# A decoder layer on one core: score products on 128 rows, probabilities as fp16 subnormals, and the tile loop written out

## The chip, the core and the metric

One core of a Trainium2 chip runs the whole kernel as one launch. Its engines work side by side and meet at semaphores: TensorE (PE, with PEld for its weight loads), VectorE (DVE), ScalarE (ACT), GpSimd (POOL), and SyncE (SP), which here only issues transfers. The metric is the device time of one execution in microseconds, lower being better.

## The reference, cut to what matters

2048 tokens of width 256 go through three sublayers, each behind a layernorm and added to its input: a self-attention across the 16 heads of one token (so its "scores" are 16 x 16 per token), a cross attention of 2048 queries on 2048 context tokens, and a mixture of 8 experts with 2 chosen. The change lies in the cross attention:

```python
q = _fq_sym(q * scale, axis=-1)          # each query's 16 numbers rounded to 127 steps
k = _fq_sym(k, axis=-1)
v = _fq_sym(v, axis=2)
attn = softmax(einsum('bhqd,bhkd->bhqk', q, k))
attn = _fq_unsigned(attn, axis=-1)       # each row rounded to 0..255, the largest is 255
out = einsum('bhqk,bhkd->bhqd', attn, v)
out = out @ Wp + bp
```

## The kernel before, in words

The tokens are cut into 16 tiles of 128. Keys and values of the context are computed, quantised and kept in SBUF once, in the first 119 us. Then every engine runs its own `body(t)` for t = 0 to 17: tile t is in cross attention, while the same body prepares tiles a = t + 2 and n = t + 1 (layernorm, self-attention, queries) and finishes m = t - 1 and o = t - 2 (output projection, experts). A body has 16 steps h, one for each head; which piece of the other tiles goes into which step is written by hand, and every engine takes its pieces strictly in that order.

One head h of tile t passes four engines. PE multiplies the queries with the keys in two halves of 1024 keys (`scores(h, i, t)`, two matmuls of 512 columns each). The operand `queries` holds two heads on top of each other; a head takes 48 rows from row 0 or from row 64 (a number of 16 is split in three bfloat16 parts, so 3 x 16 rows). DVE turns each half into scaled scores with their minimum (`keep_scores`) and makes the exponent's offset (`bias`). ACT takes the exponential (`exp_head`) and writes 0 to 255. SP issues the transposing transfer of that head from `prob` to `prob_t`. After a lag of 5 steps, PE multiplies the turned probabilities of two heads at a time with the values (`times_values`, in the odd steps between the two halves of the scores). `ps_score` has two halves, so PE may start half i of a head when DVE has read the same half of the head before. `score`, `prob` and `prob_t` are rings of 4 heads.

The 8-bit probability is written as the low byte of a 16-bit float whose high byte is that of 1024, so the number read is 1024 + p. The surplus is taken out on PE: `values4` holds sums over four blocks of values, and `neg1024` is a matrix of -1024. For every four blocks there is one matmul with these two beside the four with the probabilities.

POOL has the self-attention of tile a. In body t it works, in this order: `value_products` 2 and 3 of tile n (step 0, 1), `norm_ho` (step 2, waits for `reduce_values` 3, which DVE has in step 3), `rope` (3), `ln_scale(2, m)` (4, waits for DVE's step 6), `score_products` 0 and 1, `ln_scale(1, n)`, `score_products` 2, `choose(m)` (the experts of m, line 516 is its end), `score_products` 3, `shift_scores`, `value_products` 0 and 1. ACT's `route` waits for the end of `choose`. In step 13 it stands behind `keep_queries(n)` and `keep_routed` with `head_exp(a)`, for which POOL's `value_products` wait. DVE's `reduce_scores` 3 of tile a stands in step 13 as well.

The bodies of t = 3 to 12 are a loop with two bodies in it, run five times; those of 0 to 2 and 13 to 17 are written out. In the loop the values that a wait compares with are worked out in registers.

Of the kernel before, what the change touches and what calls it, by code (L numbers as in the profile page):

```python
# [36 lines left out]
F32 = mybir.dt.float32  # L37
BF16 = mybir.dt.bfloat16
F16 = mybir.dt.float16
U8 = mybir.dt.uint8  # L40
# [5 lines left out]
P = 128  # L46
D = 256
# [19 lines left out]
TWO_1024 = float(np.array([1024.0, 1024.0], np.float16).view(np.float32)[0])  # L67


class Tile:  # L70


    def __init__(self, idx, least, par):
        self.idx, self.least, self.par = idx, least, par

    def __add__(self, n):
        return Tile(self.idx + n, self.least + n, (self.par + n) % 2)

    def starts(self):
        return isinstance(self.idx, int) and self.idx == 0  # L80

    def exists(self):
        return not isinstance(self.idx, int) or 0 <= self.idx < T

    def starts(self):
        return isinstance(self.idx, int) and self.idx == 0

    def exists(self):
        return not isinstance(self.idx, int) or 0 <= self.idx < T

    def count(self, n, extra=0):

        return self.idx * n + extra

    def due(self, n, extra=0):

        if isinstance(self.idx, int):
            return self.idx * n + extra if self.idx * n + extra > 0 else None
        assert self.least * n + extra > 0
        return self.idx * n + extra  # L100

    def pairs(self, n, extra=0):

        return (self.idx - self.par) * (n // 2) + extra
# [12 lines left out]


def layer_kernel(nc, a):
    with ExitStack() as ctx:  # L120
# [15 lines left out]
        neg1024 = sb("neg1024", [P, P], F16)  # L136
# [29 lines left out]
        values4 = sb("values4", [P, T // 4, H // 2, 3, HD], F16)  # L166
# [19 lines left out]

        values2 = score[:, 3, 0:NTOK // 2].bitcast(F16).rearrange("p (a g j d) -> p a g j d", g=H // 2, j=2, d=HD)
# [6 lines left out]
        queries = sb("queries", [P, 2, H // 2, P], BF16)  # L194
        k_int = queries[:].rearrange("p r a q -> p (r a q)").bitcast(F32)[:, 0:2 * D].rearrange("p (h d) -> p h d", d=HD)
# [68 lines left out]
        prob_set = sem("prob_set")  # L264
# [16 lines left out]
        values_added = sem("values_added")  # L281
# [32 lines left out]
        q_kept = sem("q_kept")  # L314
        sum_inverted = sem("sum_inverted")
# [36 lines left out]
        def _(sp):  # L352
# [8 lines left out]
            load_x(Tile(0, 0, 0))  # L361
# [12 lines left out]
            load_x(Tile(1, 1, 1))  # L374
# [30 lines left out]
            load_x(Tile(2, 2, 0))  # L405

            sp.wait_ge(v_turned, T // 4)
            over_tiles(sp, body)
# [4 lines left out]
        def _(pool):  # L413
            pool.memset(ones_row[:], 1.0).then_inc(const_made, 1)
            pool.memset(minus_half[:], -0.5).then_inc(const_made, 1)
            pool.memset(neg1024[:], -1024.0).then_inc(const_made, 1)
            pool.memset(values[:, :, :, 1, :].rearrange("p a g d -> p (a g) d"), 0.0).then_inc(zeros_set, 1)
            pool.memset(values4[:, :, :, 1, :].rearrange("p a g d -> p (a g) d"), 0.0).then_inc(zeros_set, 1)
            pool.wait_ge(const_made, 3)
# [191 lines left out]
            first, second = Tile(0, 0, 0), Tile(1, 1, 1)  # L611
# [12 lines left out]
            pool.wait_ge(k_split, T // 2)  # L624
            pool.memset(prob[:, 2:4].bitcast(F32), TWO_1024).then_inc(prob_set, 1)
# [7 lines left out]
            ln_scale(0, Tile(2, 2, 0))  # L633
# [3 lines left out]
            over_tiles(pool, body)  # L637
# [3 lines left out]
        def _(act):  # L641
# [9 lines left out]
            def high_part_of_keys(u):  # L651
# [5 lines left out]
                if u == 0:  # L657
                    act.wait_ge(rows_set, 3)
# [77 lines left out]
            def keep_queries(t):  # L736
# [4 lines left out]
                act.copy(queries[:, t.par].rearrange("p a q -> p (a q)"), bank_bf[5]).then_inc(q_kept, 1)  # L741

            def exp_head(h, t):
# [5 lines left out]
                if h == 2 and t.starts():  # L749
                    act.wait_ge(prob_set, 1)  # L750
# [4 lines left out]
                act.activation(prob[:, s, :].bitcast(U8)[:, 0::2], score[:, s, :], ACT.Exp,  # L755
# [97 lines left out]
            first, second = Tile(0, 0, 0), Tile(1, 1, 1)  # L853
# [25 lines left out]
            over_tiles(act, body)  # L879
# [3 lines left out]
        def _(dve):  # L883
            def quantise_keys(u):
# [3 lines left out]
                step = Tile(u, u, 0)  # L888
# [62 lines left out]
            def round_values():  # L951
# [13 lines left out]

            def add_values():

                dve.wait_ge(values_ready, T // 4)
                dve.wait_ge(k_product, T // 2)
                dve.wait_ge(vt_product, T // 2)  # L970
                v = values[:].rearrange("p (a b) g j d -> p a b g j d", b=2)
                for j in range(0, 3, 2):
                    dve.tensor_tensor(values2[:, :, :, j // 2, :].rearrange("p a g d -> p a g d"), v[:, :, 0, :, j, :],
                                      v[:, :, 1, :, j, :], ALU.add).then_inc(values_added, 1)
                dve.wait_ge(values_added, 2)
                v = values2.rearrange("p (a b) g j d -> p a b g j d", b=2)
                for j in range(2):
                    dve.tensor_tensor(values4[:, :, :, 2 * j, :], v[:, :, 0, :, j, :], v[:, :, 1, :, j, :], ALU.add
                                      ).then_inc(values_added, 1)
# [696 lines left out]
```

## Time and profile before

| | |
|---|---|
| median of 3 runs | 1199.38 us (1195.58 to 1200.67) |
| the profiled execution, its own time | 1197.12 us |
| its span, first to last instruction | 1195.3 us |
| PE matmul busy | 945.0 us (79%) |
| DVE busy | 977.3 us (82%) |
| ACT busy | 743.7 us (62%) |
| POOL busy | 754.0 us (63%) |
| mean granted TensorE clock | 0.774 of 2.4 GHz |

A busy share is an average over the whole span. No engine is at 100%, so the waits have to be read: which engine waited for which, and where in a tile. The granted clock of a stretch is 1.00 at 2.4 GHz and 0.50 at 1.2 GHz.

### The profile page before, as it was taken

To read this page: it belongs to the slowest core of one execution; us is meant where nothing else is said; L and a number is where in the kernel's file an instruction comes from. 1 tells how busy PE (TensorE), PEld (TensorE's weight loads), DVE (VectorE), ACT (ScalarE), POOL (GpSimd) and SP (SyncE) were. 2 spreads that over 40 slices of the span, in tenths; PEclk is the share of its full clock that TensorE was granted. 3 is DMA by queue.
4 is the path that set the end of the run, shared out by engine and by line. 5 is a ranking of instruction groups with operands and counts; after the bars stand their busy time and mean duration, and the time that the engine had idled before them with its cause. 6 is when DMAs were issued, how large, how long until landed. Compare 5 with 4: busy or idle time off the path is not lost. (4 is left out here: it accounts for less than half of the span.)

```text
span 1195.3 us, 25897 instructions
## 1 busy us (share of the span) xinstructions
PE 945.0 (79%) x8256; PEld 516.1 (43%) x8256; DVE 977.3 (82%) x1944; ACT 743.7 (62%) x971; POOL 754.0 (63%) x794
## 2 busy tenths in 40 slices
PE   6765678989896868888797978787787869788874
PEld 3434233544453434444444444444444434444443
DVE  5986979888897969888798879798797979788762
ACT  2443546666777665676667766666557677668562
POOL 6537787767767675777677667767677777711011
PEclk9876667768688877787786868887687979677687
DMA  6001577769787867697896977687687968679780
GB/s 206 1 36 40 99 135 132 127 118 168 125 151 116 147 117 123 127 132 136 126 168 116 152 115 140 117 146 127 114 147 124 168 121 152 121 136 144 132 146 10
DMA packets 541061, 148.24 MB, mean 124 GB/s; under 512 B 534130, under 2 KB 538868, under 8 KB 540532
## 3 DMA queue, kind: packets, MB, share of 16 engines
q1 hardware_dynamic: 540916, 146.44, 69.8%
q8 instruction: 74, 1.21, 0.4%
q14 instruction: 71, 0.58, 0.1%
HBM read 10.09 MB, written 2.10 MB: 10 GB/s over the span
## 5 line engine op out<-in xcount | busy, mean ns | idle before, releaser
L1071 DVE TENSOR_SCALAR_CACHE_REDUCE score<-ps_score,q_neg 128x1024 f32<-128x1024 f32 x512 | 640.8, 1279 | 110.1 <-PE ps_score L1423 95.2
L755 ACT ACTIVATE prob<-score,exp_bias 128x2048 uint8<-128x2048 f32 x256 | 512.4, 2002 | 148.9 <-DVE exp_bias L1081 148.5
L1423 PE MATMUL ps_score<-keys,queries 48*128 48x512 bf16 x1024 | 369.4, 457 | 105.6 <-DVE score L1071 93.2
L1445 PE MATMUL ps_pv<-prob_t,values 128*32 128x128 f16 x4096 | 213.8, 260 | 0.0
L547 POOL TENSOR_TENSOR product<-hs_exp,v_tok 128x1024 f32<-128x1024 f32 x64 | 183.0, 2860 | 36.8 <-ACT hs_exp L728 36.7
L553 POOL TENSOR_TENSOR folded<-product 128x512 f32<-128x512 f32 x128 | 163.2, 1275 | 43.6 <-POOL product L547 33.8
L1445 PEld LDWEIGHTS ps_pv<-prob_t,values 128*32 128x32 f16 x4096 | 182.8, 119 | 0.0
L1423 PEld LDWEIGHTS ps_score<-keys,queries 48*128 48x128 bf16 x1024 | 61.8, 99 | 256.2 <-DVE score L1071 186.7
L547 POOL TENSOR_TENSOR product<-qk_rot 128x1024 f32<-128x1024 f32 x64 | 150.7, 2355 | 2.6 <-issue 1.4
L1441 PE MATMUL ps_pv<-neg,values 128*32 128x128 f16 x1024 | 136.1, 259 | 11.5 <-DMA prob_t<-prob 11.3
L784 ACT ACTIVATE routed_both<-normed,routed_gate 128x256 bf16<-128x256 f32 x124 | 52.6, 496 | 89.6 <-POOL routed_gate L516 89.6
L1441 PEld LDWEIGHTS ps_pv<-neg,values 128*32 128x32 f16 x1024 | 62.6, 115 | 89.6 <-issue 89.6
L429 POOL TENSOR_SCALAR var_eps<-mean_var 128x1 f32<-128x1 f32 x48 | 12.1, 252 | 106.8 <-DVE mean_var L990 83.5
L1490 PE MATMUL ps<-ident_bf,routed_both 128*128 128x128 bf16 x256 | 27.3, 271 | 46.8 <-ACT routed_both L784 27.5
L1296 PEld LDWEIGHTS ps<-routed_both,w 128*128 128x128 bf16 x512 | 40.4, 122 | 40.6 <-issue 34.3
L1081 DVE TENSOR_SCALAR exp_bias<-low 128x1 f32<-128x1 f32 x256 | 52.9, 206 | 4.0
L998 DVE TENSOR_REDUCE hs<-folded 128x64 f32<-128x256 f32 x64 | 26.4, 414 | 34.8 <-POOL folded L558 34.8
L558 POOL TENSOR_TENSOR folded<-folded 128x256 f32<-128x256 f32 x64 | 47.5, 743 | 11.4 <-POOL folded L553 11.4
L1296 PE MATMUL ps<-routed_both,w 128*128 128x128 bf16 x512 | 53.1, 269 | 1.9 <-DVE early L1134 1.8
L755 ACT ACTIVATION_READ_ACCUMULATOR prob<-score,exp_bias 128x1 f32 x256 | 48.5, 189 | 0.0
L460 POOL TENSOR_TENSOR ho_n<-ho,hs_inv 128x256 f32<-128x256 f32 x16 | 10.0, 622 | 60.7 <-DVE ho L1020 60.7
L707 ACT COPY normed_t<-ps 128x256 f32<-128x256 f32 x48 | 17.6, 367 | 46.5 <-PE ps L1301 46.5
(136 smaller groups left out, 1276.8 us busy)
## 6 DMA issues: line engine op xcount, KB each, us to landing
prob_t<-prob SPq DMA_TRANSPOSE x256, 4.5
prob_t<-in_w SPq DMA_DIRECT2D x3, 1024.0 KB, 4.8
x_in<-in_x SPq DMA_DIRECT2D x16, 128.0 KB, 2.7
score<-in_cond_t SPq DMA_DIRECT2D x4, 512.0 KB, 7.1
out<-x_out SPq DMA_DIRECT2D x16, 128.0 KB, 2.4
w_qkv<-in_w_qkv SPq DMA_DIRECT2D x1, 768.0 KB, 4.1
early<-in_w_kv SPq DMA_DIRECT2D x1, 512.0 KB
w_s<-in_w_s SPq DMA_DIRECT2D x3, 128.0 KB
```

Source lines behind the costliest of these rows:

```text
L547: pool.tensor_tensor(product[:, r], a_, b_, ALU.mult).then_inc(multiplied, 1)
L553: pool.tensor_tensor(folded[:, r], product[:, r, :, :, 0:HD // 2], product[:, r, :, :, HD // 2:HD], ALU.add).then_inc(fold_done, 1)
L558: pool.tensor_tensor(folded[:, r, :, :, 0:HD // 4], folded[:, r, :, :, 0:HD // 4], folded[:, r, :, :, HD // 4:HD // 2], ALU.add).then_inc( ...
L755: act.activation(prob[:, s, :].bitcast(U8)[:, 0::2], score[:, s, :], ACT.Exp, bias=exp_bias[:, s:s + 1], scale=-1.0, accum_out=prob_sum[:, ...
L784: act.activation(routed[:, e, :], normed[:, 2, :], ACT.Copy, scale=routed_gate[:, e:e + 1]).then_inc(routed_done[i], 1)
L1071: dve.tensor_scalar(score[:, s, HALF * i:HALF * i + HALF], ps_score[:, i].rearrange("p b k -> p (b k)"), q_neg[:, t.par, h:h + 1], None, A ...
L1081: dve.tensor_scalar(exp_bias[:, s:s + 1], low[:, s, 0:1], low[:, s, 1:2], LN255, ALU.min, ALU.add).then_inc(bias_ready, 1)
L1296: mm = pe.matmul(out, lhs[c], rhs[c], start=start and c == 0, stop=stop and c == C - 1)
L1423: mm = pe.matmul(ps_score[:, i, b, :], queries[lo:lo + 3 * HD, t.par, h // 2, :], keys[lo:lo + 3 * HD, h // 2, k0:k0 + KEYS], start=True, ...
L1441: pe.matmul(out[j], beside_zeros(values4, i, h + j), neg1024[:], start=(i == 0 and first), stop=False)
L1445: mm = pe.matmul(out[j], beside_zeros(values, 4 * i + b, h + j), prob_t[:, (h + j) % RING, 4 * i + b, :], start=False, stop=(i == T // 4 - ...
L1490: mm = pe.transpose(bank_bf[6 + i][:, P * j:P * j + P], routed[:, EG * i + e, P * c:P * c + P], ident_bf[:])
```

## The change

Three things are changed, all in how the cross attention is carried out; the layer's result is the same function.

1. `queries` gets a further dimension j: block j holds the queries of head 2a + j in its own 64 rows, and zeros in the other 64 rows, set once. A score product takes all 128 rows of `queries` and of `keys`. `keep_queries` is two copies of 64 rows in place of one of 128.
2. The exponential writes a 16-bit integer 0 to 255, which read as a 16-bit float is the subnormal p x 2^-24; `w_p` is multiplied by 2^24 once. `neg1024`, `values4`, `add_values` and their 1024 matmuls go.
3. `over_tiles` is a Python loop over all 18 bodies, so no engine branches back and every wait compares with a constant.

```diff
@@ over_tiles
-def over_tiles(eng, body):
-    for t in range(3):
-        body(Tile(t, t, t % 2))
-    with eng.Fori(3, T - 4, 2) as t:
-        body(Tile(t, 3, 1))
-        body(Tile(t + 1, 4, 0))
-    for t in range(T - 3, T + 2):
-        body(Tile(t, t, t % 2))
+def over_tiles(body):
+    for t in range(T + 2):
+        body(Tile(t))
@@ buffers
-        queries = sb("queries", [P, 2, H // 2, P], BF16)
+        queries = sb("queries", [P, 2, H // 2, 2, P], BF16)
@@ gpsimd
-            pool.wait_ge(k_split, T // 2)
-            pool.memset(prob[:, 2:4].bitcast(F32), TWO_1024).then_inc(prob_set, 1)
+            pool.wait_ge(k_chain, 6 * (T // 2))
+            pool.memset(queries[:].rearrange("p r a j q -> p (r a j q)").bitcast(F32), 0.0).then_inc(rows_cleared, 1)
@@ keep_queries
-                act.copy(queries[:, t.par].rearrange("p a q -> p (a q)"), bank_bf[5]).then_inc(q_kept, 1)
+                if t.starts():
+                    act.wait_ge(rows_cleared, 1)
+                for j in range(2):
+                    rows = slice(P // 2 * j, P // 2 * j + P // 2)
+                    act.copy(queries[rows, t.par, :, j, :], bank_bf[5][rows, :].rearrange("p (a q) -> p a q", q=P)
+                             ).then_inc(q_kept, 1)
@@ exp_head
-                act.activation(prob[:, s, :].bitcast(U8)[:, 0::2], score[:, s, :], ACT.Exp,
+                act.activation(prob[:, s, :].bitcast(U16), score[:, s, :], ACT.Exp,
@@ round_values
-                    dve.tensor_scalar(w_p[:, c, :], w_p[:, c, :], v_scale[:, c:c + 1], None, ALU.mult
+                    dve.tensor_scalar(w_p[:, c, :], w_p[:, c, :], v_scale[:, c:c + 1], 1.0 / UNIT, ALU.mult, ALU.mult
@@ vector, tile 0, step 0
-                            add_values()
@@ scores
-                    mm = pe.matmul(ps_score[:, i, b, :], queries[lo:lo + 3 * HD, t.par, h // 2, :],
-                                   keys[lo:lo + 3 * HD, h // 2, k0:k0 + KEYS], start=True, stop=True)
+                    mm = pe.matmul(ps_score[:, i, b, :], queries[:, t.par, h // 2, h % 2, :],
+                                   keys[:, h // 2, k0:k0 + KEYS], start=True, stop=True)
@@ times_values
-                for i in range(T // 4):
-                    for j in range(2):
-                        pe.matmul(out[j], beside_zeros(values4, i, h + j), neg1024[:],
-                                  start=(i == 0 and first), stop=False)
-                    for b in range(4):
-                        for j in range(2):
-                            mm = pe.matmul(out[j], beside_zeros(values, 4 * i + b, h + j),
-                                           prob_t[:, (h + j) % RING, 4 * i + b, :], start=False,
-                                           stop=(i == T // 4 - 1 and b == 3 and last))
+                for i in range(T):
+                    for j in range(2):
+                        mm = pe.matmul(out[j], beside_zeros(values, i, h + j), prob_t[:, (h + j) % RING, i, :],
+                                       start=(i == 0 and first), stop=(i == T - 1 and last))
```

The changes of place can be seen in the order of instructions. On PE, step 5 of tile 0, from the first half of that step's scores (the last two of the four products in the first row are of step 4) to the second half's. Before:

```order
L1296 MATMUL ps<-w_qkv,normed_t 128x256 x2
L1423 MATMUL ps_score<-keys,queries 128x512 x2
L1441 MATMUL ps_pv<-neg,values 32x128 x2
L1445 MATMUL ps_pv<-prob_t,values 32x128 x8
L1441 MATMUL ps_pv<-neg,values 32x128 x2
L1445 MATMUL ps_pv<-prob_t,values 32x128 x8
L1441 MATMUL ps_pv<-neg,values 32x128 x2
L1445 MATMUL ps_pv<-prob_t,values 32x128 x8
L1441 MATMUL ps_pv<-neg,values 32x128 x2
L1445 MATMUL ps_pv<-prob_t,values 32x128 x8
L1423 MATMUL ps_score<-keys,queries 128x512 x2
```

And with the change, at the same place:

```order
L1256 MATMUL ps<-w_qkv,normed_t 128x256 x2
L1382 MATMUL ps_score<-keys,queries 128x512 x2
L1400 MATMUL ps_pv<-prob_t,values 32x128 x32
L1382 MATMUL ps_score<-keys,queries 128x512 x2
L1256 MATMUL ps<-w_qkv,normed_t 128x256 x2
```

The block of products between the two halves goes from 40 matmuls to 32, and nothing else changes its place. On DVE, step 0 of tile 0, from its scores to the scores of step 1. Before:

```order
L1071 TENSOR_SCALAR score,low<-ps_score,q_neg 128x1024 x2
L985 BN_STATS stats<-x_in 128x6
L1081 TENSOR_SCALAR exp_bias<-low 128x1
L973 TENSOR_TENSOR score<-values 128x64x16 x2
L978 TENSOR_TENSOR values<-score 128x32x16 x2
L998 TENSOR_REDUCE hs<-folded 128x64
L963 CAST w<-prob_t 128x2048
```

And with the change:

```order
L1033 TENSOR_SCALAR score,low<-ps_score,q_neg 128x1024 x2
L949 BN_STATS stats<-x_in 128x6
L1043 TENSOR_SCALAR exp_bias<-low 128x1
L962 TENSOR_REDUCE hs<-folded 128x64
L942 CAST w<-prob_t 128x2048
```

The four additions ahead of `reduce_scores` (the first `hs`) are gone.

## Rows read from the trace of the kernel before

**Rows 1.** The page's span, and its granted clock in 40 slices of the span, in tenths.

```profile
span 1195.3 us, 25897 instructions
...
PEclk9876667768688877787786868887687979677687
```

**Rows 2.** Waits of DVE: total us, times, longest; whole span.

```profile
DVE score L1071 <- PE ps_score L1423: 95.2, 88, 5.2
DVE hs L998 <- POOL folded L558: 34.8, 11, 4.4
DVE score L1071 <- issue: 12.9, 8, 5.3
```

**Rows 3.** Timeline at the start of tile 5: start, duration, engine; [idle before].

```profile
448.11 1.28 DVE L1071 TENSOR_SCALAR_CACHE_REDUCE score<-ps_score,q_neg 128x1024 f32<-128x1024 f32 x1 [5.34 <-issue]
...
453.41 0.22 POOL L429 TENSOR_SCALAR var_eps<-mean_var 128x1 f32<-128x1 f32 x1 [5.36 <-issue]
```

**Rows 4.** POOL's timeline: the end of `choose` in bodies 1, 4, 5, 6, 13.

```profile
232.88 0.21 POOL L516 TENSOR_TENSOR routed_gate<-gate 128x8 f32<-128x8 f32 x1 [0.18 <-POOL gate L513]
...
429.11 0.21 POOL L516 TENSOR_TENSOR routed_gate<-gate 128x8 f32<-128x8 f32 x1 [0.18 <-POOL gate L513]
...
497.98 0.21 POOL L516 TENSOR_TENSOR routed_gate<-gate 128x8 f32<-128x8 f32 x1 [0.18 <-POOL gate L513]
...
562.34 0.21 POOL L516 TENSOR_TENSOR routed_gate<-gate 128x8 f32<-128x8 f32 x1 [0.18 <-POOL gate L513]
...
1021.01 0.21 POOL L516 TENSOR_TENSOR routed_gate<-gate 128x8 f32<-128x8 f32 x1 [0.18 <-POOL gate L513]
```

**Rows 5.** ACT's timeline in body 5, from that end of `choose`.

```profile
498.22 1.71 ACT L784 ACTIVATE routed_both<-normed,routed_gate 128x256 bf16<-128x256 f32 x4 [6.13 <-POOL routed_gate L516]
...
505.55 0.99 ACT L741 COPY queries<-ps 128x1024 bf16<-128x1024 bf16 x1
...
507.35 0.42 ACT L728 ACTIVATE hs_exp<-hs 128x256 f32<-128x256 f32 x1
```

**Rows 6.** DVE and POOL, from step 13 of body 5 to step 3 of body 6.

```profile
503.28 0.42 DVE L998 TENSOR_REDUCE hs<-folded 128x64 f32<-128x256 f32 x1 [3.57 <-POOL folded L558]
...
525.88 1.26 POOL L553 TENSOR_TENSOR folded<-product 128x512 f32<-128x512 f32 x1 [0.27 <-POOL product L547]
...
530.22 0.68 DVE L1020 TENSOR_REDUCE ho<-folded 128x64 f32<-128x512 f32 x1
```

**Rows 7.** DVE and PE around step 15 of body 5 and steps 1 and 3 of body 6.

```profile
506.88 0.29 PE L1441 MATMUL ps_pv<-neg,values 128*32 128x128 f16 x2
...
509.13 1.03 PE L1423 MATMUL ps_score<-keys,queries 48*128 48x512 bf16 x2
...
510.20 1.28 DVE L1071 TENSOR_SCALAR_CACHE_REDUCE score<-ps_score,q_neg 128x1024 f32<-128x1024 f32 x1 [1.60 <-PE ps_score L1423]
...
515.08 0.23 PE L1441 MATMUL ps_pv<-neg,values 128*32 128x128 f16 x2 [0.83 <-DMA prob_t<-prob]
...
516.31 0.60 PE L1423 MATMUL ps_score<-keys,queries 48*128 48x512 bf16 x2
...
526.51 1.28 DVE L1071 TENSOR_SCALAR_CACHE_REDUCE score<-ps_score,q_neg 128x1024 f32<-128x1024 f32 x1 [0.96 <-PE ps_score L1423]
...
528.76 1.28 DVE L1071 TENSOR_SCALAR_CACHE_REDUCE score<-ps_score,q_neg 128x1024 f32<-128x1024 f32 x1 [0.96 <-PE ps_score L1423]
```

**Rows 8.** PE in three stretches of bodies 5 and 6: length, busy, granted clock, DMA.

```profile
500.00:510.40 10.40, 8.18 (x68) 0.51 0.67 94
541.10:547.90 6.80, 5.39 (x58) 1.00 1.17 190
551.30:565.00 13.70, 13.51 (x103) 0.50 0.57 115
```

**Rows 9.** DVE's timeline, `add_values` in step 0 of tile 0.

```profile
121.65 2.55 DVE L973 TENSOR_TENSOR score<-values 128x1024 f16<-128x1024 f16 x2
124.23 0.76 DVE L978 TENSOR_TENSOR values<-score 128x512 f16<-128x512 f16 x2
```

**Rows 10.** Waits of DVE from 1026 to 1160 us, the last tiles.

```profile
DVE score L1071 <- PE ps_score L1423: 19.6, 18, 2.7
```

More of the change, by code:

```diff
@@ L65, with __init__ @@
 FLOOR = 1e-8
-TWO_1024 = float(np.array([1024.0, 1024.0], np.float16).view(np.float32)[0])
+UNIT = 2.0 ** -24
 class Tile:
-    def __init__(self, idx, least, par):
-        self.idx, self.least, self.par = idx, least, par
+    def __init__(self, idx):
+        self.idx, self.par = idx, idx % 2
     def __add__(self, n):
-        return Tile(self.idx + n, self.least + n, (self.par + n) % 2)
+        return Tile(self.idx + n)
     def starts(self):
-        return isinstance(self.idx, int) and self.idx == 0
+        return self.idx == 0
     def exists(self):
[L83 to L89, printed above, removed]
+        return 0 <= self.idx < T
     def count(self, n, extra=0):
@@ L609, in body @@
                         value_products(h - 14, a)
-            first, second = Tile(0, 0, 0), Tile(1, 1, 1)
+            first, second = Tile(0), Tile(1)
             ln_scale(0, first)
@@ L850, in body @@
                         exp_head(h, t)
-            first, second = Tile(0, 0, 0), Tile(1, 1, 1)
+            first, second = Tile(0), Tile(1)
             ln_apply(0, x_in[:, 0, :], first)
@@ L877, in _ @@
             keep_values(3)
-            over_tiles(act, body)
+            over_tiles(body)
         @block.vector
@@ L1064, in keep_scores @@
                             dve.wait_ge(k_product, T // 2)
-                        if t.starts() and h == 3:
-                            dve.wait_ge(values_added, 4)
                         if (due := t.due(H, h - RING + 1)) is not None:
@@ L1243, in body @@
                             largest_score(a)
-            first, second = Tile(0, 0, 0), Tile(1, 1, 1)
+            first, second = Tile(0), Tile(1)
             loaded(first)
@@ L1251, in _ @@
             dve.memset(q_parts[:], 0.0).then_inc(rows_set, 1)
-            dve.memset(prob[:, 0:2].bitcast(F32), TWO_1024).then_inc(rows_set, 1)
-            dve.wait_ge(rows_set, 3)
+            dve.wait_ge(rows_set, 2)
             for u in range(T // 2 + 2):
@@ L1287, in _ @@
             reduce_scores(0, second)
-            over_tiles(dve, body)
+            over_tiles(body)
         @block.tensor
@@ L1501, in experts @@
                     if (t + 2).exists():
[L1503 removed]
+                        pe.wait_ge(q_kept, (t + 2).count(2, 2))
                 if i == 1 and j == 1:
@@ L1582, in body @@
                             experts(0, 0, m)
-            first, second = Tile(0, 0, 0), Tile(1, 1, 1)
+            first, second = Tile(0), Tile(1)
             ln_turn(0, first)
@@ L1614, in _ @@
             q_turn(first)
-            over_tiles(pe, body)
+            over_tiles(body)
 def kernel(x, ctx_2048, L0_attn_Wq, L0_attn_Wk, L0_attn_Wv, L0_attn_Wo, L0_xattn_Wq, L0_xattn_bq,
```

63 lines of the change are left out of this document (19 added, 44 removed).

## The prediction

> **What bounds the kernel now.** I read the page first. It has a span of 1195.3 us, and a granted clock that never stays at full or at half for long [rows 1]. DVE is busiest, so I asked next what DVE waits for: 95.2 us for score products of PE in 88 waits, 34.8 us for POOL's folded products in 11 waits, and 12.9 us for "issue", that is for nothing the profile shows, in 8 waits [rows 2]. These three belong to three different limits.
>
> The "issue" waits lie where a loop goes round. At the start of tile 5, DVE stands for 5.34 us, and POOL stands for 5.36 us a little later [rows 3]. The loop runs five times, so there are four such places, at tiles 5, 7, 9 and 11.
>
> For the rest I needed the length of a tile and a marker that is not blurred. I took the end of `choose` on POOL [rows 4]. From body 4 to 5 it is 68.87 us, with a loop-back in it, and from 5 to 6 it is 64.36 us, without one. From body 1 to body 13 it is 788.1 us, 12 tiles. Twelve times 64.4 is 772.8, and the four with a loop-back hold the other 15.3 us; so a loop-back costs 3.8 us net, not 5.3, because other waits of the tile shrink meanwhile.
>
> Then I followed one tile without a loop-back, 64.4 us, from `choose` to `choose` [rows 5, 6]:
> - `choose` ends at 498.2; ACT, which had waited 6.13 us for it, works without a gap to `head_exp` at 507.35: 9.2 us.
> - POOL's last value product is folded at 527.1: 19.8 us.
> - DVE takes it up at 530.2 (`reduce_values` 3, step 3): 3.1 us later. This is the only slack in the ring.
> - From there to the next end of `choose`, 562.5: 32.3 us. In it DVE works for steps 3 to 6 and then POOL without any wait to the end of `choose`.
>
> The reader is to see that POOL and ACT, with 63% and 62% busy, close the ring in all but 3.1 us. DVE confirms it: in step 13 it waits 3.57 us for POOL [rows 6]. The waits of DVE for PE count only as far as they lie between step 13 and step 3: 1.60 us in step 15, and 0.96 and 0.96 in step 3, together 3.5 us [rows 7]. Those in steps 9 and 11 are given back at step 13.
>
> **The loop written out.** Four loop-backs at 3.8 us net: 15 us gained. The bodies that are straight code already (0 to 2, 13 to 17) show no wait for "issue" that matters, so I charge nothing for fetching straight code. Register arithmetic is off: below 0.5 us a tile, taken as nothing.
>
> **Fewer value products.** At the low clock the 40 products between the two halves of a head's scores take 2.25 us (506.88 to 509.13), and at the high clock 1.23 us (515.08 to 516.31) [rows 7]. 32 in place of 40 take off a fifth: 0.45 or 0.25 us. Two such blocks lie on DVE's way between steps 13 and 3 (steps 15 and 3), so 0.9 us a tile at the low clock. Whether a product with subnormal numbers takes longer no row shows. Its bounds are nothing, and a large loss, if it were handled as slowly as fp32, which I price below. I take nothing, since the array gets operands of the same type and shape.
>
> **All 128 rows.** The number of matmuls and their columns stay. So any effect must come by the clock. What do the rows say of it? From 551.3 to 565.0, PE was busy 13.51 of 13.70 us, and had 1.2 GHz; from 541.1 to 547.9 it was busy 5.39 of 6.80 us and had 2.4 GHz [rows 8]. So an engine busy all the time is not enough. The first stretch has mostly score products on 48 rows and value products 32 wide; the second has fp32 products on 128 rows between them. I read this as a grant that depends on how much of the array is in use, so scores on 128 rows should lift it. The pair of score products takes 1.03 us at the low clock and 0.60 at the high one [rows 7].
>
> The Trainium skill says otherwise: by "TensorE: Matmul & The Clock Gate", Part 1, the gate is set by how busy the engine has been. By that rule rows of zeros would lift nothing, and 1024 fewer matmuls would make low stretches more frequent, a result of its own, which is the second of the rivals below.
>
> Where does the lift reach? The two places that count are the worst for it. Between 500.0 and 510.4 PE itself waited (busy 8.18 of 10.40 at 0.51) [rows 8], as it stands behind `choose`, ACT's `route` and DVE's step 13. I expect the clock to come back earlier than now in some tiles and not in others. With the high clock throughout, the 3.5 us go altogether; with none, only 0.9.
>
> **The second copy.** `keep_queries` is one copy of 0.99 us, with `head_exp` behind it [rows 5]. A copy's time goes by the elements of a row, which stay 1024, so the second adds some 1.0 us, and in the ring that is fully on the path: 9.2 becomes 10.2. It is bounded by half a copy if rows count (0) and by 1.0. I take 1.0.
>
> **What stands at the end of it.** The ring is now 10.2 + 19.8 + 32.3 = 62.3 us without any slack: a tile can't be shorter. On DVE's side it is 64.4 less what is recovered of the 3.5: 63.5 with the shorter blocks alone. I take 62.9, midway, since the clock rises in part. For 12 tiles that is 754.8 in place of 788.1 us: 33.3 us gained, the loop-backs included.
>
> **Start and end.** `add_values` takes 3.3 us of DVE ahead of work that POOL waits for [rows 9]; with 0.9 us for the second copy ahead of the first scores, 2.5 us are gained. Behind body 13 POOL has little left, so DVE's waits for PE are on the path: 19.6 us in 18 waits [rows 10]. Of these I take 8: 0.45 for most blocks, and the clock for the rest. The memset that clears `queries` is as large as the one of `prob` that it replaces, and it starts earlier.
>
> **Sum:** 33.3 + 2.5 + 8 = 43.8 us. The profiled execution has 1197.1 us, so 1153.3; it lies 2.3 us under the median of the runs, so I forecast 1155 us.
>
> **The rivals.**
> - *All waits for PE vanish* (the clock is high nearly everywhere). For it: a stretch fully busy was at the low clock, so there is much to win. Against it: PE waits itself in steps 13 to 15. POOL and ACT are then the ring: 12 x 62.3 = 747.6, 40.5 gained, 14 at the end, 2.5 at the start: 1142 us. Chance 0.18.
> - *The grant follows busy time alone.* Then the clock sinks a little as matmuls go, and what the shorter blocks save, low stretches take back: 12 tiles of 64.4 = 772.8, 15.3 gained, 2.5 at the start, 2 at the end: 1179 us. It is spoken against by the busy stretch at half clock [rows 8]. Chance 0.14.
> - *Nothing but the loop is gained, and the copies eat it*: 15 gained, 16 x 1.0 lost: 1200 us beside the median, the change doing nothing for the time. It would need DVE to be late at step 3 for another reason. Chance 0.03.
> - *Slower: straight code stalls at every tile.* If engines that no longer repeat code had to wait for it once in each tile as they now do at a loop-back, 16 times 3.8 us come on top of the forecast: 1216 us. It decides from 2.8 us a tile on (43.8 by 16). Against it: the straight bodies now have no such wait. With it I count products slowed by subnormals: at four times their time a block would grow by 3 us or more, and the time by hundreds. Chance for both 0.05.
>
> The forecast itself has 0.60, with a range of its own from 1146 to 1168.
>
> **How the numbers follow.** A change of up to 0.5% (6 us) can't be told from none here. Faster by more: the first three cases, 0.92. Within it: 0.03. Slower: 0.05. The range leaves out the last two cases and the part of the second that is faster still, so it runs from 1138 (all waits gone and a cheap second copy) to 1180.
>
> **What would show it.** No wait for "issue" of over 1 us on DVE behind the first body. A granted clock between 0.82 and 0.90 over the span; under 0.78 the clock follows busy time alone. DVE's waits for score products at 40 to 60 us. The marker `choose` at steps of 62.3 to 63.5 us; if it is 62.3 in each, POOL and ACT are the bound, and DVE waits for POOL at `ho` in step 3 too. `queries` with 32 copies of about 1 us. DVE's wait for POOL at `hs` stays at 3 to 4 us a tile. I am wrong if tiles come under 62 us, since then the ring has a link that I took as rigid and that isn't, most likely the 32.3 us; or if the value products get longer.

## The result, and the profile after

The changed kernel takes 1142.8 us (median of 4 runs, 1141.5 to 1144.0), the kernel before on the same chip 1198.6 us (4 runs, 1195.6 to 1200.7). The ratio is 0.9536, with a 95% interval from 0.9512 to 0.956: faster by 56 us. The forecast was 1155 us with a range from 1138 to 1180. So the range holds the time; but the forecast's own narrower range (1146 to 1168) doesn't, and the number of the first rival, 1142 us, is the one that was met.

The page of the changed kernel: span, busy time of each engine, and the granted clock in 40 slices.

```profile
span 1140.6 us, 21740 instructions
...
PE 772.9 (68%) x7110; PEld 460.5 (40%) x7232; DVE 947.2 (83%) x1939; ACT 758.7 (67%) x987; POOL 752.4 (66%) x792
...
PEclk9877778979798979879798988898888989898986
```

Against [rows 1], sixes have become eights and nines: the mean granted clock goes from 0.774 to 0.862. DVE, the busiest engine, is busy 30 us less. TensorE's busy time is understated here, since the trace lacks 122 of its 7232 matmuls; exp_first below, with the same matmuls and all of them on record, has 789.1 us, some 156 us less than before.

The waits of DVE: total, times, longest.

```profile
DVE hs L962 <- POOL folded L532: 69.7, 24, 5.1
DVE score L1033 <- PE ps_score L1382: 37.3, 41, 3.2
...
DVE ho L984 <- POOL folded L527: 10.1, 16, 1.0
```

Against [rows 2], the wait for score products falls from 95.2 us to 37.3, and the waits for "issue" of over 1 us are gone. The wait for POOL at `hs` has doubled, from 34.8 to 69.7 us: DVE now arrives in step 13 early in every tile, and what it arrives early for is POOL's chain.

POOL's timeline, the end of `choose` in bodies 1, 4, 5, 6 and 13, as in [rows 4].

```profile
229.25 0.21 POOL L490 TENSOR_TENSOR routed_gate<-gate 128x8 f32<-128x8 f32 x1 [0.18 <-POOL gate L487]
...
416.83 0.20 POOL L490 TENSOR_TENSOR routed_gate<-gate 128x8 f32<-128x8 f32 x1 [0.18 <-POOL gate L487]
...
479.37 0.20 POOL L490 TENSOR_TENSOR routed_gate<-gate 128x8 f32<-128x8 f32 x1 [0.18 <-POOL gate L487]
...
541.90 0.20 POOL L490 TENSOR_TENSOR routed_gate<-gate 128x8 f32<-128x8 f32 x1 [0.18 <-POOL gate L487]
...
979.09 0.21 POOL L490 TENSOR_TENSOR routed_gate<-gate 128x8 f32<-128x8 f32 x1 [0.18 <-POOL gate L487]
```

These rows split the gain. Up to body 1 it is 3.6 us (232.9 to 229.25), over the 12 tiles 38.3 us (788.1 to 749.8), and behind them 12.8 us (174.3 to 161.5 up to the end of the span). All 12 tiles lie between 62.2 and 62.7 us; no tile is longer for a loop-back.

The ring of body 5, first on ACT, then on POOL, then on DVE, as in [rows 5, 6].

```profile
479.61 1.71 ACT L763 ACTIVATE routed_both<-normed,routed_gate 128x256 bf16<-128x256 f32 x4 [6.62 <-POOL routed_gate L490]
...
486.94 2.02 ACT L719 COPY queries<-ps 64x1024 bf16<-64x1024 bf16 x2
488.99 1.01 ACT L770 COPY routed_both<-ps 128x1024 bf16<-128x1024 bf16 x1
489.89 0.42 ACT L702 ACTIVATE hs_exp<-hs 128x256 f32<-128x256 f32 x1
```

```profile
508.38 1.27 POOL L527 TENSOR_TENSOR folded<-product 128x512 f32<-128x512 f32 x1 [0.27 <-POOL product L521]
```

```profile
484.34 0.42 DVE L962 TENSOR_REDUCE hs<-folded 128x64 f32<-128x256 f32 x1 [4.57 <-POOL folded L532]
...
510.05 0.68 DVE L984 TENSOR_REDUCE ho<-folded 128x64 f32<-128x512 f32 x1
```

From the end of `choose` (479.6) to `head_exp` (489.9) it is 10.3 us, to the last folded product (509.65) 19.8, to DVE's `ho` 0.4, and to the next end of `choose` (542.1) 32.1. The sum is 62.5. The slack of 3.1 us has shrunk to 0.4, which is what closes the ring. Body 5 still has some slack; in most of the 12 tiles there is none, and DVE waits 0.4 to 0.6 us for POOL at that `ho`. (In the kernel before, the slack in the 12 tiles ran from nothing, behind one loop-back, to 4.4 us; the 3.1 us are one tile's.)

### The profile page after: what moved, and what is told of

Same layout as the page of the kernel before. It is cut to its first block and busy times, and to the rows that moved or that the text cites. A ratio compares the mean times of both kernels' runs of the same rounds, so it can differ in the third digit from the quotient of the medians.

```text
span 1140.6 us, 21740 instructions
## 1 busy us (share of the span) xinstructions
PE 772.9 (68%) x7110; PEld 460.5 (40%) x7232; DVE 947.2 (83%) x1939; ACT 758.7 (67%) x987; POOL 752.4 (66%) x792
## 5 line engine op out<-in xcount | busy, mean ns | idle before, releaser
L1033 DVE TENSOR_SCALAR_CACHE_REDUCE score<-ps_score,q_neg 128x1024 f32<-128x1024 f32 x512 | 638.0, 1278 | 38.2 <-PE ps_score L1382 37.3
L734 ACT ACTIVATE prob<-score,exp_bias 128x2048 uint16<-128x2048 f32 x256 | 511.4, 1999 | 96.1 <-DVE exp_bias L1043 95.7
L1382 PE MATMUL ps_score<-keys,queries 128*128 128x512 bf16 x902 | 311.8, 424 | 150.2 <-DVE score L1033 127.2
L527 POOL TENSOR_TENSOR folded<-product 128x512 f32<-128x512 f32 x128 | 163.3, 1275 | 40.8 <-POOL product L521 30.5
L1400 PE MATMUL ps_pv<-prob_t,values 128*32 128x128 f16 x4096 | 158.8, 239 | 45.1 <-DMA prob_t<-prob 45.0
L1400 PEld LDWEIGHTS ps_pv<-prob_t,values 128*32 128x32 f16 x4096 | 135.0, 106 | 109.8 <-issue 109.8
L1382 PEld LDWEIGHTS ps_score<-keys,queries 128*128 128x128 bf16 x1024 | 71.4, 104 | 256.9 <-DVE score L1033 221.8
L962 DVE TENSOR_REDUCE hs<-folded 128x64 f32<-128x256 f32 x64 | 26.5, 416 | 69.8 <-POOL folded L532 69.7
L1444 PEld LDWEIGHTS ps<-ident_bf,routed_both 128*128 128x128 bf16 x256 | 21.2, 124 | 86.6 <-ACT routed_both L763 85.3
L1256 PE MATMUL ps<-routed_both,w 128*128 128x128 bf16 x512 | 46.6, 246 | 7.0 <-ACT routed_both L770 5.7
L984 DVE TENSOR_REDUCE ho<-folded 128x64 f32<-128x512 f32 x64 | 42.8, 669 | 10.1 <-POOL folded L527 10.1
L1033 DVE DVE_READ_ACCUMULATOR score<-ps_score,q_neg 128x1 f32 x512 | 42.1, 82 | 0.0
L501 POOL TENSOR_TENSOR qk_sin<-qk,rope_sin 128x256 f32<-128x256 f32 x32 | 27.1, 868 | 17.5 <-ACT qk L689 16.6
## 6 DMA issues: line engine op xcount, KB each, us to landing
w_qkv<-in_w_qkv SPq DMA_DIRECT2D x1, 768.0 KB, 4.3
```

Of the source, the lines that this page charges most:

```text
L527: pool.tensor_tensor(folded[:, r], product[:, r, :, :, 0:HD // 2], product[:, r, :, :, HD // 2:HD], ALU.add).then_inc(fold_done, 1)
L734: act.activation(prob[:, s, :].bitcast(U16), score[:, s, :], ACT.Exp, bias=exp_bias[:, s:s + 1], scale=-1.0, accum_out=prob_sum[:, t.par, ...
L984: dve.tensor_reduce(ho[:, G * j:G * j + G, :], folded[:, j % 2], AX.X, ALU.add).then_inc(reduced, 1)
L1033: dve.tensor_scalar(score[:, s, HALF * i:HALF * i + HALF], ps_score[:, i].rearrange("p b k -> p (b k)"), q_neg[:, t.par, h:h + 1], None, A ...
L1256: mm = pe.matmul(out, lhs[c], rhs[c], start=start and c == 0, stop=stop and c == C - 1)
L1382: mm = pe.matmul(ps_score[:, i, b, :], queries[:, t.par, h // 2, h % 2, :], keys[:, h // 2, k0:k0 + KEYS], start=True, stop=True)
```

## The experiments

Each edit is against the changed kernel unless it says otherwise. Each kernel was timed beside the kernel before on its chip, whose medians were 1200.2 us (first four experiments), 1200.3 (next three) and 1204.9 (last three), so between groups the ratios are to be compared. "12 tiles" is again the time from `choose` of body 1 to that of body 13.

| kernel | median, us | ratio to before, 95% | clock | start, 12 tiles, end, us |
|---|---|---|---|---|
| rows48 | 1178.8 | 0.9825 (0.9774 to 0.9877) | 0.700 | 236.3, 768.0, 174.1 |
| rows64 | 1165.8 | 0.9726 (0.968 to 0.9772) | 0.758 | 234.5, 760.2, 165.2 |
| third_copy | 1159.6 | 0.9665 (0.9617 to 0.9712) | 0.858 | 231.6, 761.1, 166.0 |
| exp_first | 1134.1 | 0.9454 (0.9407 to 0.9501) | 0.872 | 229.7, 740.5, 163.0 |
| straight_only | 1181.5 | 0.9864 (0.9783 to 0.9946) | 0.778 | 232.1, 769.1, 174.3 |
| all_but_rows | 1172.6 | 0.9805 (0.9733 to 0.9878) | 0.706 | 234.1, 762.0, 174.8 |
| change_in_loop | 1180.0 | 0.9838 (0.9771 to 0.9905) | 0.857 | 229.8, 786.7, 163.3 |
| only_tensor_loops | 1174.4 | 0.9757 (0.9713 to 0.9801) | 0.855 | 229.0, 782.5, 161.6 |
| only_tensor_straight | 1167.9 | 0.9714 (0.9672 to 0.9756) | 0.862 | 229.1, 773.6, 161.4 |
| exp_first_in_before | 1198.5 | 0.9966 (0.9937 to 0.9996) | 0.771 | 233.2, 791.4, 170.2 |

**How many rows a score product uses.** The buffer with its zeros and both copies stay; only the slice that the product reads changes, to the 48 rows that hold a head's numbers or to its 64.

```diff
-                    mm = pe.matmul(ps_score[:, i, b, :], queries[:, t.par, h // 2, h % 2, :],
-                                   keys[:, h // 2, k0:k0 + KEYS], start=True, stop=True)
+                    lo = 64 * (h % 2)
+                    mm = pe.matmul(ps_score[:, i, b, :], queries[lo:lo + 48, t.par, h // 2, h % 2, :],
+                                   keys[lo:lo + 48, h // 2, k0:k0 + KEYS], start=True, stop=True)
```

> The changed kernel, but each score product takes only the 48 rows of its own head (queries and keys sliced again), with the new layout, both copies and everything else kept. If the grant of the clock depends on how much of the array is in use: mean granted clock back to 0.76 to 0.79, DVE waits for scores up from 37 to 70 us or more, tiles at 63.5 us instead of 62.5, and the time 1155 to 1165 us. If the grant follows busy time alone: clock 0.86 as in the changed kernel, and 1143 us.

> As the kernel with 48 rows, but with 64 rows (16 of them hold zeros). If use of the array sets the clock: between 48 and 128 rows and near the former, clock 0.78 to 0.81, 1150 to 1162 us. If busy time alone: 0.86 and 1143 us. If what counts is whether both halves of the rows are taken, 64 rows are like 48.

The clock is 0.700 with 48 rows, 0.758 with 64 and 0.862 with 128, and the time 1178.8, 1165.8 and 1142.8 us. DVE's waits for score products go with it: 103.4, 78.5 and 37.3 us. Both expectations had the order right and the size too small (0.76 to 0.79 for 48 rows, 0.78 to 0.81 for 64), and both times came out above their ranges. The rival that only the halves of the rows count, so that 64 rows are like 48, is out: 0.758 against 0.700, and the runs of the two (1162 to 1167 us and 1175 to 1181 us) lie apart. The three kernels issue the same matmuls with the same columns in the same order. One stretch of rows48: length, then the busy time of PE, PEld, DVE, ACT and POOL, the granted clock, the DMA share and GB/s.

```profile
792.00:804.00 12.00, 12.00 (x81) 6.37 (x82) 10.36 (x23) 8.79 (x12) 10.34 (x11) 0.50 0.85 163
```

TensorE works without a pause here and has 1.2 GHz, like the stretch in [rows 8]. Its page, over the whole span:

```profile
PE 995.6 (84%) x7232; PEld 521.3 (44%) x7232; DVE 974.0 (83%) x1939; ACT 761.3 (65%) x987; POOL 750.3 (64%) x792
...
PEclk9877555668685858668595859585767778667675
```

The kernel with the busiest TensorE (84%; 80% with 64 rows, about 70% with 128) has the lowest clock. And 128 rows cost nothing by themselves: the pair of products took 1.03 us at the low and 0.60 at the high clock with 48 rows [rows 7], and with 128 rows:

```profile
486.99 1.04 PE L1382 MATMUL ps_score<-keys,queries 128*128 128x512 bf16 x2 [0.43 <-DVE score L1033]
487.95 1.89 PE L1400 MATMUL ps_pv<-prob_t,values 128*32 128x128 f16 x32
489.77 0.60 PE L1382 MATMUL ps_score<-keys,queries 128*128 128x512 bf16 x2
```

**The loop alone.** The kernel before with its bodies written out, nothing else.

```diff
-    for t in range(3):
-        body(Tile(t, t, t % 2))
-    with eng.Fori(3, T - 4, 2) as t:
-        body(Tile(t, 3, 1))
-        body(Tile(t + 1, 4, 0))
-    for t in range(T - 3, T + 2):
+    for t in range(T + 2):
         body(Tile(t, t, t % 2))
```

> The kernel before with over_tiles as a Python loop and nothing else. By the forecast's step the four loop-backs cost 3.8 us each net: 15 us gained, about 1184 us. Rival: they cost their whole 5.3 us, 1178 us; or other waits take them back, 1198 us. Clock 0.77 as before.

The 12 tiles take 769.1 us instead of 788.1: 19.0 us gained, with 0.7 us ahead of them and nothing behind them. The four tiles that had a loop-back give 15.6 of the 19.0 us (272.0 to 256.4), the other eight 3.4 us. One execution of each kernel is compared here, and the executions of either spread over 12 us and more.

**Everything but the rows and the second copy.** The changed kernel with products on 48 rows and one copy of all 128 rows into block 0 (the waits for the copies, which count one in place of two, are not shown).

```diff
-                for j in range(2):
-                    rows = slice(P // 2 * j, P // 2 * j + P // 2)
-                    act.copy(queries[rows, t.par, :, j, :], bank_bf[5][rows, :].rearrange("p (a q) -> p a q", q=P)
-                             ).then_inc(q_kept, 1)
+                act.copy(queries[:, t.par, :, 0, :], bank_bf[5].rearrange("p (a q) -> p a q", q=P)).then_inc(q_kept, 1)
...
-                    mm = pe.matmul(ps_score[:, i, b, :], queries[:, t.par, h // 2, h % 2, :],
-                                   keys[:, h // 2, k0:k0 + KEYS], start=True, stop=True)
+                    lo = 64 * (h % 2)
+                    mm = pe.matmul(ps_score[:, i, b, :], queries[lo:lo + 48, t.par, h // 2, 0, :],
+                                   keys[lo:lo + 48, h // 2, k0:k0 + KEYS], start=True, stop=True)
```

> Straight code and subnormal probabilities, but score products on 48 rows and one copy of 128 rows in keep_queries, so all of the change but its rows. The forecast's step put this at 63.5 us a tile and about 1165 us with the clock as before, 0.77. After the run with 48 rows and two copies (1179 us, clock 0.70) I expect a clock near 0.70 too, since the 1024 full-row products of the old scheme are gone, and 1170 to 1178 us: the second copy matters little where DVE, not POOL, closes the ring. If the second copy is fully on the path it is 1163 to 1166 us.

Beside straight_only, the page of each of the two kernels, straight_only first:

```profile
PE 937.6 (80%) x8256; PEld 513.8 (44%) x8256; DVE 961.9 (82%) x1944; ACT 742.1 (63%) x971; POOL 752.9 (64%) x794
...
PEclk9776667878697968888796959587887959578675
```

```profile
PE 988.6 (84%) x7232; PEld 517.5 (44%) x7232; DVE 968.2 (83%) x1939; ACT 744.1 (64%) x971; POOL 750.7 (64%) x792
...
PEclk9877555657585767668586858595778878757575
```

TensorE has 1024 matmuls fewer and is busy 51 us longer. The clock sinks from 0.778 to 0.706. The products that went were those with `neg1024`, on all 128 rows, so products on 48 rows are a larger share of what is left; that this is the reason fits the runs with 48 and 64 rows, but is argued. Taking the correction out gains only 9 us between the medians, with intervals of the two ratios that overlap, so it can't be told from nothing. Whether the missing products or the small numbers lowered the clock wasn't tried separately; both came with this step. This kernel and rows48 (0.9805 and 0.9825) differ by the second copy alone, and the difference can't be told from none.

**The ring on ACT.** Two kernels: a third copy of 64 rows into a buffer that nobody reads (its buffer and the counts of the waits are not shown), and `head_exp(a)` ahead of `keep_queries(n)` and `keep_routed` in step 13.

```diff
                     act.copy(queries[rows, t.par, :, j, :], bank_bf[5][rows, :].rearrange("p (a q) -> p a q", q=P)
                              ).then_inc(q_kept, 1)
+                act.copy(spare[0:P // 2], bank_bf[5][0:P // 2, :].rearrange("p (a q) -> p a q", q=P)
+                         ).then_inc(q_kept, 1)
```

```diff
+                    if a.exists() and h == 13:
+                        head_exp(a)
                     if n.exists() and h == 13 + late:
                         keep_queries(n)
                     if m.exists() and h in (13, 14):
                         keep_routed(h - 13, m)
-                    if a.exists() and h == 13:
-                        head_exp(a)
```

> The changed kernel with a third copy of 64 rows in keep_queries, into a buffer nobody reads, ahead of head_exp. If the ring of choose, ACT, value products on POOL and DVE's step 3 to 6 has no slack: every tile is 1.0 us longer (63.5 us), 12 to 14 us in all, 1156 us. If DVE's waits for scores bound the tile: no change, 1143 us.

> The changed kernel with head_exp(a) moved ahead of keep_queries and keep_routed on ACT in step 13; no work is added or removed. The ring theory: head_exp starts up to 2.9 us earlier, then DVE is the next limit; DVE's 1.1 us of waiting for POOL in steps 2 and 3 go, so tiles of about 61.4 us and 1130 us. Rival: queries come 0.4 us later and routed_turn 0.4 us later, PE is late at step 0 and DVE loses what the ring gains: 1143 us.

The third copy stands ahead of `head_exp` as meant:

```profile
493.88 2.02 ACT L720 COPY queries<-ps 64x1024 bf16<-64x1024 bf16 x2
495.93 1.01 ACT L722 COPY spare<-ps 64x1024 bf16<-64x1024 bf16 x1
```

The 12 tiles take 11.3 us more: 0.94 us a tile for a copy of 1.01 us, so ACT's stretch is on the path. The start takes 2.4 us more and the end 4.5. That is 18.1 us between the profiled executions and 16.8 us between the medians, more than the 12 to 14 us that were expected, since the start and the end pay too.

In exp_first, `head_exp` comes 3.0 us sooner behind its `routed_both` pair:

```profile
485.76 0.19 ACT L734 ACTIVATION_READ_ACCUMULATOR prob<-score,exp_bias 128x1 f32 x1
485.85 0.40 ACT L702 ACTIVATE hs_exp<-hs 128x256 f32<-128x256 f32 x1
486.16 2.02 ACT L719 COPY queries<-ps 64x1024 bf16<-64x1024 bf16 x2
```

But the tiles shrink by 0.8 us, not by 3: `ho` in step 3 now finds its product ready 1.4 to 4.2 us before DVE comes to it, so DVE sets the tile again. With 1134.1 us it is the fastest kernel here, 9 us under the changed one.

**The same move in the kernel before**, where the ring has 3.1 us of slack.

> The kernel before with ScalarE's head_exp ahead of keep_queries and keep_routed in step 13, the same move that gave 8.7 us in the changed kernel. Theory of the ring: here DVE reaches reduce_values 3 some 3.1 us after POOL has folded it, so an earlier start of POOL's value products meets a slack and gives nothing: 1197 to 1201 us, and tiles of 64.4 as before. Rival: the move pays by itself, by taking DVE's wait at step 13 or POOL's idle time, whether or not there is slack: 9 us or more gained, 1191 us or less.

The 12 tiles take 791.4 us (788.1 before), and the ratio is 0.9966 (0.9937 to 0.9996), under half a per cent. POOL's last folded product and `ho_n`, then DVE's `ho`:

```profile
524.95 1.26 POOL L553 TENSOR_TENSOR folded<-product 128x512 f32<-128x512 f32 x1 [0.28 <-POOL product L547]
...
531.48 0.62 POOL L460 TENSOR_TENSOR ho_n<-ho,hs_inv 128x256 f32<-128x256 f32 x1 [5.28 <-DVE ho L1020]
```

```profile
530.44 0.68 DVE L1020 TENSOR_REDUCE ho<-folded 128x64 f32<-128x512 f32 x1
```

The product is ready at 526.2, 0.9 us sooner than in [rows 6], and DVE comes for it at 530.4, no sooner than there. In this tile the slack grew from 3.1 to 4.2 us, and DVE came no sooner.

**The loop back in the changed kernel.** `over_tiles` as it was, with its waits on registers.

> The changed kernel with the five-times loop and its register waits put back. If the ring has no slack left, each of the four loop-backs costs its whole 5.3 us: 21 us, 1164 us. If they cost 3.8 us as before: 1158 us.

It costs 36 us against the changed kernel (ratios 0.9838 and 0.9536), not the 21 that were expected. The four tiles with a loop-back take 70.4 to 72.2 us, the others 62.6. The wait that makes them long is not DVE's, but TensorE's. Its first products in such a tile:

```profile
439.03 0.63 PE L1400 MATMUL ps_score<-keys,queries 128*128 128x512 bf16 x1 [8.19 <-issue]
...
572.76 0.63 PE L1400 MATMUL ps_score<-keys,queries 128*128 128x512 bf16 x1 [8.68 <-issue]
```

Two more kernels ask whose stand this is: the loop on TensorE alone, and on all engines but it (in each, the other side has all 18 bodies written out with waits on constants).

```diff
-            over_tiles(pe, body)
+            for u in range(T + 2):
+                body(Tile(u, u, u % 2))
```

> The counterpart: the changed kernel with the loop on TensorE alone, all other engines written out. Theory (the stand is TensorE's own): PE stands 8.2 to 8.9 us at each of four loop-backs, with or without the other engines' loops, so 4 x 8.5 on 1142.8: 1177 us. Rival: the stand is as long as it is because five engines fetch their code at once; alone TensorE would stand about the 4.3 us that it had at one loop-back of the kernel before: 1160 us or less.

> The changed kernel with the five-times loop on every engine but TensorE, whose bodies are all written out. With all five in the loop the four tiles with a loop-back took 70.4 to 72.2 us where the others take 62.6, and PE stood 8.2 to 8.9 us for nothing that the trace shows ahead of the first score product of such a tile. Theory: that stand is TensorE's own way back to the start of its code. Then it goes, and what is left is the way back of DVE and POOL, 5.3 us in the kernel before and now without slack around it: loop-back tiles of 66 to 68 us, 1156 to 1164 us. Rival one: the other engines' ways back are hidden, and only TensorE's counts: 1143 us. Rival two: the stand belongs to the loop of all engines (one that waits for the others): nothing changes, 1180 us.

With the loop on TensorE alone, it stands 7.2 to 7.7 us at each of the four places, and these tiles take 70.6 to 71.0 us:

```profile
435.94 1.03 PE L1404 MATMUL ps_score<-keys,queries 128*128 128x512 bf16 x2 [7.15 <-issue]
...
702.83 1.03 PE L1404 MATMUL ps_score<-keys,queries 128*128 128x512 bf16 x2 [7.71 <-issue]
```

So the stand is TensorE's own; the loops of the other engines add about 1 us to it. With the loop on the others alone the tiles take 67.3 to 68.2 us. At the start of each, POOL stands 4.5 to 5.2 us in two pieces for nothing that the trace shows. DVE waits 3.4 to 4.3 us there, one time for "issue" and three times, as the trace has it, for ScalarE. The rows at the second place:

```profile
566.30 1.28 DVE L1051 TENSOR_SCALAR_CACHE_REDUCE score<-ps_score,q_neg 128x1024 f32<-128x1024 f32 x1 [4.33 <-issue]
...
574.47 0.57 POOL L425 TENSOR_TENSOR rstd<-var_eps,minus_half 128x1 f32<-128x1 f32 x1 [2.98 <-issue]
```

Over the 12 tiles the changed kernel has 749.8 us, the loop on the others adds 23.8, on TensorE 32.7, and on all 36.9: they lie mostly beside each other and do not add up. With the loop on TensorE alone the time of 1174.4 us is near the 1177 that were expected. With it on the others the time of 1167.9 us is above the expected 1156 to 1164: the way back costs 5.9 us a tile there, against 3.8 in the kernel before. In the kernel before, TensorE's longest wait for "issue" at such a place was 4.3 us. Why TensorE's is longer in the changed kernel stays open; it has fewer instructions between the two ends, not more.

## Why the prediction was right, and where it was not

**The ring.** Right, link by link. 10.2 + 19.8 + 32.3 were forecast, 10.3 + 19.8 + 32.1 measured, with 0.4 us of slack in body 5 (0.6 forecast, as 62.9 less 62.3) and none in most other tiles. Three kernels hold it up: a third copy costs 0.94 us a tile, moving `head_exp` pays in the changed kernel, and it pays nothing in the kernel before, where the slack takes it. DVE's wait at `hs` was forecast at 3 to 4 us a tile and was 4.6 in the tile shown; its waits for score products were forecast at 40 to 60 us and were 37.3.

**The loop.** 15.3 us forecast, and 15.6 measured in the four tiles where it alone is changed; the other 3.4 of the 19.0 us lie in tiles without a loop-back and can't be told from the spread of the runs. In the changed kernel undoing it costs 36.9 us over the 12 tiles. So 3.8 us was the price in the kernel before and not a fixed one: without the slack, the way back of the engines other than TensorE costs 5.9 us a tile (23.8 by 4), and TensorE's own stand of over 7 us, whose reason is open, brings it to 9.2. The 36.9 us are 21 more than in the kernel before, over half of what the rows gave.

**Fewer value products, subnormals.** The block of 32 was forecast to take a fifth off 2.25 and 1.23 us. From the first product of a block to the next score product, the median over the blocks is 1.82 us at the low clock (19 blocks) and 1.00 at the high one (96), of 128 blocks, so 32 fortieths to within 2%; the row at 487.95 above is one of the first kind. Products with subnormals take no longer. ACT's exponential to 16 bits takes 1999 ns, as long as to 8 bits (2002). What the forecast missed is that this part, by itself, brings a lower clock: 0.778 to 0.706. The second rival had foretold a sinking clock, though for another reason: by it a less busy TensorE is granted less, and here TensorE was busier. Its size was met by no term of the sum, and only the rows cover it.

**All 128 rows.** Right in kind: the grant depends on how many rows of the array a product uses. (Other ways to use more of it, such as more columns of weights, were not tried.) The reading that led to it was thin: the low stretch from 551.3 us, which was told as score products on 48 rows and value products, also has fp32 products on 128 rows, 3.9 of its 13.5 busy us, against 2.6 of 5.4 in the high one from 541.1 us. That is a difference of degree in two stretches and could not have shown it; the runs with 48 and 64 rows do. The clock of 0.862 lies in the forecast's 0.82 to 0.90, and rows48, busier and colder, rules out that busy time alone decides. The Trainium skill has the gate set by how busy TensorE has been ("TensorE: Matmul & The Clock Gate", Part 1). The runs with 48, 64 and 128 rows go against it as the only thing that counts: busy 84%, 80% and about 70% of the span, they were granted 0.700, 0.758 and 0.862. Wrong in size: the step that failed is the one on where the lift reaches. I took 62.9 us for a tile, midway between 63.5 and the floor of 62.3, since PE itself waits in steps 13 to 15. It does, and the score products of step 15 are still at the low clock in the rows above (1.04 us), and DVE still waits there, 0.83 us instead of 1.60. In step 3 it waits 0.54 and 0.25 us instead of twice 0.96 [rows 7]. And a wait of 0.72 us in step 1 is new. DVE's waits for scores from step 13 to step 3:

```profile
490.41 1.28 DVE L1033 TENSOR_SCALAR_CACHE_REDUCE score<-ps_score,q_neg 128x1024 f32<-128x1024 f32 x1 [0.83 <-PE ps_score L1382]
...
499.74 1.28 DVE L1033 TENSOR_SCALAR_CACHE_REDUCE score<-ps_score,q_neg 128x1024 f32<-128x1024 f32 x1 [0.72 <-PE ps_score L1382]
...
507.06 1.28 DVE L1033 TENSOR_SCALAR_CACHE_REDUCE score<-ps_score,q_neg 128x1024 f32<-128x1024 f32 x1 [0.54 <-PE ps_score L1382]
...
508.60 1.28 DVE L1033 TENSOR_SCALAR_CACHE_REDUCE score<-ps_score,q_neg 128x1024 f32<-128x1024 f32 x1 [0.25 <-PE ps_score L1382]
```

The new one has its cause on PE, whose value products of step 1 stood 2.54 us for their operand:

```profile
496.85 1.89 PE L1400 MATMUL ps_pv<-prob_t,values 128*32 128x128 f16 x32 [2.54 <-DMA prob_t<-prob]
```

So 3.5 us became 2.3, and from `hs` to `ho` DVE takes 25.7 us instead of 26.9, 1.2 less. The rest of the 1.9 us between 64.4 and 62.5 comes in small pieces: 0.3 from `choose` to `hs` (5.1 to 4.8), and 0.3 from `ho` to `choose` (32.3 to 32.05). I had 1.5 in all. At the end I took 8 us for DVE's 19.6 us of waits [rows 10]; it was 12.8, of the 14 that the first rival gave it. Over 12 tiles the gain was 38.3 and not 33.3 us, so these two sizes make 10 of the 12 us between forecast and result. Of the rows' whole gain (rows48 against the changed kernel: 35 to 36 us by ratios and medians, 37.8 between the profiled executions), 18.2 lie in the 12 tiles, 12.6 behind them and 7.1 ahead.

**The start.** 2.5 us were forecast and 3.6 measured. The additions stood where the forecast had them: POOL reaches the same product at 120.7 us in both kernels, and before the change it then waited 2.46 us for the `hs` that DVE has behind `add_values`. At POOL's `ho_n` in step 2 of body 1 the changed kernel is 3.9 us ahead. Before and after:

```profile
125.50 2.06 POOL L553 TENSOR_TENSOR folded<-product 128x512 f32<-128x512 f32 x1 [2.46 <-DVE hs L998]
...
202.27 0.62 POOL L460 TENSOR_TENSOR ho_n<-ho,hs_inv 128x256 f32<-128x256 f32 x1 [1.94 <-DVE ho L1020]
```

```profile
123.31 1.25 POOL L527 TENSOR_TENSOR folded<-product 128x512 f32<-128x512 f32 x1 [0.27 <-POOL product L521]
...
198.33 0.62 POOL L434 TENSOR_TENSOR ho_n<-ho,hs_inv 128x256 f32<-128x256 f32 x1 [1.09 <-DVE ho L984]
```

DVE had also begun its first scores 4.6 us sooner (114.1 against 118.8), so the missing additions and this head start can't be told apart. What the forecast left out is the clock. The kernel all_but_rows has the same lead at that `ho_n` and loses it, and more, in waits before `choose`:

```profile
198.59 0.62 POOL L434 TENSOR_TENSOR ho_n<-ho,hs_inv 128x256 f32<-128x256 f32 x1 [1.11 <-DVE ho L981]
...
202.77 1.65 POOL L501 TENSOR_TENSOR qk_sin<-qk,rope_sin 128x256 f32<-128x256 f32 x2 [3.09 <-ACT qk L689]
...
212.47 0.22 POOL L403 TENSOR_SCALAR var_eps<-mean_var 128x1 f32<-128x1 f32 x1 [5.37 <-DVE mean_var L951]
```

From 199 to 229 us its clock is 0.67 and that of the changed kernel 0.94. The stretch from 119 us to body 1's `choose`, in rows48 and in the changed kernel:

```profile
119.00:236.00 117.00, 97.59 (x577) 44.25 (x578) 90.62 (x183) 64.88 (x76) 89.11 (x82) 0.56 0.71 124
```

```profile
119.00:229.00 110.00, 68.27 (x610) 35.99 (x620) 93.18 (x193) 63.74 (x76) 88.89 (x82) 0.82 0.74 132
```

A clock of 0.56 against 0.82, and 7 us. So the changed kernel keeps its lead because the rows hold the clock up; with the subnormals and the straight loop alone it is gone.

**The rivals.** That all waits for PE vanish is not what happened, though its 1142 us is: 37.3 us of them are left, and those of steps 15 and 3 are still in the ring's tile. It was right in that POOL and ACT now close the ring. The others (busy time alone, the copies eating the gain, straight code stalling in each tile) are out: by the runs with 48 and 64 rows, by the gain of 56 us itself, and by the waits for "issue", of which none on DVE is over 1 us.

## What to carry to other kernels

Before putting zeros or doubled operands aside as waste, look at the granted clock of the stretches in which TensorE is always busy. If they stand at 1.2 GHz, products that use more of the rows at the same columns may be worth more than fewer products, and cutting work may lose the clock.

A wait read from a kernel with slack is a lower bound of its price. Find the ring and its slack first: the same move of `head_exp` was worth nothing with 3.1 us of slack and 9 us with 0.4, and a loop-back went from about 4 us to 6 on the engines other than TensorE (to 9 with TensorE's own stand, whose reason is open).

Split a change on the chip by its parts and put each part back into the whole. Between the medians the loop alone gives 19 us, the missing products and subnormals about 9, the second copy takes 6 (neither can be told from nothing), and the rows on top give 36; the loop put back takes 36 to 37 away.

## What the runs showed of the hardware

- The size of the rows' effect: 0.700, 0.758 and 0.862 of 2.4 GHz for 48, 64 and 128 rows in 1024 score products among 7232 matmuls, 64 of the 128 rows holding only zeros in `queries`. The forecast had the direction, not the size.
- TensorE stands 7.2 to 8.9 us when its code branches back, in the changed kernel, even if all other engines run straight. DVE stood 5.3 and 4.9 us in the kernel before and 4.3 us once with the loop on all but TensorE. In the kernel with all 18 bodies straight, DVE's longest wait for "issue" behind 119 us is 0.2 us.
- ScalarE's copy of 64 rows x 1024 takes 1.01 us, one of 128 rows 0.99: splitting a copy by rows doubles it, as the forecast took it.
- At the higher clock of the changed kernel TensorE comes to its value products before their operand does. It waited 11.3 us for `prob_t` before and 45.0 us now, the longest 3.0. In the tile shown, 0.7 us of such a wait reaches DVE.
